# Two planes by expert for the results of an expert layer, each read back when its own tiles have landed

## What is computed

```python
x = x + tanh(g_xattn[0]) * _L0_xattn_ref(...)
x = x + tanh(g_ffn[0])   * _L0_ffn_ref(...)
x = x + tanh(g_xattn[1]) * _L1_xattn_ref(...)
x = x + tanh(g_ffn[1])   * _L1_ffn_ref(_layernorm(x), W_gate, b_gate, W_e, b_e)

def _L1_ffn_ref(x, W_gate, b_gate, W_e, b_e):
    logits = x @ W_gate + b_gate
    _, top_idx = jax.lax.top_k(logits, 2)
    y_all = jax.nn.relu(jnp.einsum('bsd,edh->bseh', x, W_e) + b_e)
    return jnp.take_along_axis(y_all, top_idx[..., None], axis=2).mean(axis=2)
```

## Time and profile before

| | us |
|---|---|
| runs shown | 986.0, 989.31, 989.25 |
| their median | 989.25 |
| the profiled execution, its own time | 989.37 |
| its span, first to last instruction | 987.3 |
| PE busy in it | 896.6 |
| DVE busy in it | 617.9 |

### The profile page before, as it was taken

How to read it: one execution, slowest core, us unless ns; L and a number is a source line. 1 busy time by engine, 2 the same in 40 slices (tenths; PEclk the granted TensorE clock), 3 DMA queues, 4 the chain that set the end, 5 groups by cost and what they waited for, 6 DMA issues and landing times.

```text
span 987.3 us, 13859 instructions
## 1 busy us (share of the span) xinstructions
PE 896.6 (91%) x4771; PEld 732.7 (74%) x4771; DVE 617.9 (63%) x1063; ACT 320.6 (32%) x572; POOL 409.3 (41%) x418
## 2 busy tenths in 40 slices
PE   4799999999999899999999999798999998668991
PEld 4677878978878877878977867575888885656770
DVE  5776575375674276575375665478888875875335
ACT  4423133223133224133223133012665664612330
POOL 4453342152442153352152333337765606546540
PEclk9899999999999999999999999799999996579995
DMA  8020120020020010020020020302344206323437
GB/s 306 12 76 11 33 86 1 11 86 2 33 86 1 13 54 32 33 86 1 11 80 6 1 76 1 108 1 58 101 131 144 67 2 220 128 75 118 139 128 287
DMA packets 42306, 70.13 MB, mean 71 GB/s; under 512 B 7098, under 2 KB 14843, under 8 KB 42115
## 3 DMA queue, kind: packets, MB, share of 16 engines
q1 hardware_dynamic: 37124, 56.97, 17.7%
q0 software_dynamic: 3680, 12.06, 3.6%
q10 hardware_dynamic: 1440, 0.24, 0.1%
HBM read 52.61 MB, written 10.22 MB: 64 GB/s over the span
## 4 chain that ended last, share of the span: by engine, by line
PE 76%; DVE 9%; issue 6%; POOL 5%; DMA 3%; ACT 1%; SPq 0%; POOLq 0%; DVEq 0%
PE ps L1345 17%; PE ps L1347 16%; PE ps L1346 16%; PE ps L1445 5%; PE ps L1437 5%; PE ps L1576 4%; PE ps L1453 3%; PE ps L1564 2%; POOL y_rows L639 2%; PE ps L1557 2%; POOL rows_in L630 1%; POOL k_blk L580 1%; DVE stats L894 1%; DMA rows_in<-h_rows,gather_i 1%; PE ps L1626 1%
## 5 line engine op out<-in xcount | busy, mean ns | idle before, releaser
L516 POOL TENSOR_TENSOR q_t<-rot_a,rot_b 128x512 f32<-128x512 f32 x64 | 82.7, 1292 | 155.2 <-DVE rot_b L944 155.2
L1345 PE MATMUL ps<-wo_hi,at_hi 128*128 128x512 f32 x256 | 107.2, 419 | 5.4 <-DVE at_lo L1013 5.4
L942 DVE TENSOR_TENSOR rot_a<-ps,cos 128x512 f32<-128x512 f32 x80 | 55.2, 690 | 89.6 <-PE ps L1347 89.4
L1345 PE MATMUL ps<-xt_hi,wq_hi 128*128 128x512 f32 x256 | 108.1, 422 | 0.2 <-issue 0.2
L1347 PE MATMUL ps<-xt_hi,wq_lo 128*128 128x512 f32 x256 | 101.5, 397 | 0.0
L1346 PE MATMUL ps<-xt_lo,wq_hi 128*128 128x512 f32 x256 | 101.4, 396 | 0.0
L1347 PE MATMUL ps<-wo_hi,at_lo 128*128 128x512 f32 x256 | 100.8, 394 | 0.0
L1346 PE MATMUL ps<-wo_lo,at_hi 128*128 128x512 f32 x256 | 100.3, 392 | 0.0
L748 ACT ACTIVATE ps<-ps 128x512 f32<-128x512 f32 x64 | 37.2, 582 | 177.7 <-PE ps L1437 177.7
L759 ACT ACTIVATE at_hi<-ps 128x512 fp32r<-128x512 f32 x64 | 38.2, 598 | 172.9 <-PE ps L1453 172.9
L1018 DVE TENSOR_TENSOR X<-ps,X 128x512 f32<-128x512 f32 x64 | 44.2, 691 | 77.8 <-PE ps L1347 77.4
(11 more groups left out here) (215 smaller groups left out, 2131.6 us busy)
## 6 DMA issues: line engine op xcount, KB each, us to landing
wq_raw<-in_wq SPq DMA_DIRECT2D x8, 1024.0 KB, 5.3
wo_raw<-in_wo SPq DMA_DIRECT2D x8, 1024.0 KB, 5.1
w_raw<-in_we SPq DMA_DIRECT2D x8, 1024.0 KB, 5.6
y_in<-y_rows SPq DMA_DIRECT2D x16, 256.0 KB, 5.6
X<-in_x SPq DMA_DIRECT2D x4, 512.0 KB, 13.1
wk_raw<-in_wk SPq DMA_DIRECT2D x8, 256.0 KB, 2.8
q_t<-in_ctx_t SPq DMA_DIRECT2D x2, 1024.0 KB, 10.5
wv_raw<-in_wv SPq DMA_DIRECT2D x4, 512.0 KB, 3.8
```

The source lines that it names most:

```text
L516: nc.gpsimd.tensor_tensor(dst, rot_a[:, r % 2, :], rot_b[:, r % 2, :], ALU.add).then_inc(rope_ok, 1)
L942: nc.vector.tensor_tensor(heads(rot_a[:, r % 2, :]), heads(bank), bcast(cos[:, :], 4), ALU.mult)
L1345: nc.tensor.matmul(dst, w_hi, x_hi, start=start and k == 0, stop=False)
```

## The change

Each row now has its two results in planes by expert: plane 0 takes that of the lower numbered of its two experts, plane 1 that of the higher. `slot2` is therefore made from the sum of a row's two slots, their maximum, and the difference of the two. Plane 0 never gets a row from expert 7.

For each of the two planes and each of the three semaphores `y_out[j]`, DVE works out how far the semaphore must have counted (`real`, `real_f`, `real_i`), behind `of_tile_i` and ahead of the remainders of the expert weights. SP loads the six numbers and waits on `y_out` itself; `landed` and `y_seq` are gone from POOL. SP reads plane 0 in 4 DMAs of 512 KB when tiles 0 to 18 have landed, and plane 1 in 8 of 256 KB when tiles 0 to 20 have. DVE adds plane 0 to all eight blocks, then plane 1 to all eight.

The core of the diff (the numbers of the waits on `slot_ok` behind it are one higher):

```diff
-            sp.wait_ge(real_ok, CREDIT + 1)
-            real = sp.value_load(last_real[0:1, 0:1], min_val=CREDIT + TOP * N // P, max_val=CREDIT + NT)
-            sp.wait_ge(y_seq, real)
+            sp.wait_ge(real_ok, CREDIT + TOP + 2)
+            lower_done, all_done = tiles_up_to(0), tiles_up_to(1)
+            for j in range(3):
+                sp.wait_ge(y_out[j], lower_done[j])
             for q in range(KT):
-                for b in range(2 * q, 2 * q + 2):
-                    for k in range(TOP):
-                        sp.dma_start(y_in[:, b, k, :], yv[:, b, k, :]).then_inc(y_ok[q], 16)
+                sp.dma_start(y_in[:, 2 * q:2 * q + 2, 0, :], yv[:, 2 * q:2 * q + 2, 0, :]).then_inc(yl_ok[q // 2], 16)
+            for j in range(3):
+                sp.wait_ge(y_out[j], all_done[j])
+            for b in range(B):
+                sp.dma_start(y_in[:, b, 1, :], yv[:, b, 1, :]).then_inc(y_ok[b // 2], 16)
...
-            def landed(i):
-                gp.wait_ge(y_out[i % 3], 16 * (i // 3) + 16)
-                gp.sem_inc(y_seq, 1)
...
-            nc.vector.tensor_tensor(of_rank[:, :, :, :], rank[:, :, :].unsqueeze(2).to_broadcast([P, B, TOP, EX]), by_rank,
-                                    ALU.is_equal).then_inc(slot_ok, 1)
...
-            nc.vector.tensor_tensor(of_rank[:, :, :, :], of_rank[:, :, :, :], slot[:, :, :].unsqueeze(2).to_broadcast([P, B, TOP, EX]),
-                                    ALU.mult).then_inc(slot_ok, 1)
-            ve.wait_ge(slot_ok, CREDIT + 8)
-            nc.vector.tensor_reduce(slot2[:, :].rearrange("p (b k) -> p b k", b=B), of_rank[:, :, :, :], AX.X, ALU.add).then_inc(slot_ok, 1)
+            nc.vector.tensor_tensor(slot[:, :, :], slot[:, :, :], sel[:, :, :].bitcast(F32), ALU.mult).then_inc(slot_ok, 1)
+            ve.wait_ge(slot_ok, CREDIT + 7)
+            by_expert = slot2[:, :].rearrange("p (b k) -> p k b", b=B)
+            nc.vector.tensor_reduce(both[:, :], slot[:, :, :], AX.X, ALU.add).then_inc(slot_ok, 1)
+            nc.vector.tensor_reduce(by_expert[:, 1, :], slot[:, :, :], AX.X, ALU.max).then_inc(slot_ok, 1)
             ve.wait_ge(slot_ok, CREDIT + 9)
+            nc.vector.tensor_tensor(by_expert[:, 0, :], both[:, :], by_expert[:, 1, :], ALU.subtract).then_inc(slot_ok, 1)
...
-            nc.vector.tensor_scalar(last_real[:, :], t_upto[:, EX - 1:EX], float(CREDIT), None, ALU.add).then_inc(real_ok, 1)
...
+            for n in range(TOP):
+                nc.vector.tensor_scalar(real[:, n, :], tile_no, t_upto[:, EX - TOP + n:EX - TOP + n + 1], 16.0, ALU.is_lt, ALU.mult).then_inc(real_ok, 1)
+            ve.wait_ge(real_ok, CREDIT + TOP)
+            nc.vector.tensor_reduce(real_f[:, :, :], real[:, :, :].rearrange("p k (n j) -> p k j n", j=3), AX.X, ALU.add).then_inc(real_ok, 1)
+            ve.wait_ge(real_ok, CREDIT + TOP + 1)
+            nc.vector.tensor_copy(real_i[:, :], real_f[:, :, :].rearrange("p k j -> p (k j)")).then_inc(real_ok, 1)
...
             for b in range(B):
-                ve.wait_ge(y_ok[b // 2], 64)
+                ve.wait_ge(yl_ok[b // 4], 32)
                 nc.vector.scalar_tensor_tensor(X[:, b, :], y_in[:, b, 0, :], tanh_g[:, 3:4], X[:, b, :], ALU.mult, ALU.add).then_inc(y0_ok, 1)
+            for b in range(B):
+                ve.wait_ge(y_ok[b // 2], 32)
                 ve.wait_ge(y0_ok, CREDIT + b + 1)
                 nc.vector.scalar_tensor_tensor(X[:, b, :], y_in[:, b, 1, :], tanh_g[:, 3:4], X[:, b, :], ALU.mult, ALU.add).then_inc(x4_ok, 1)
```

More of the change, by code:

```diff
@@ L207, in flamingo_gated_two_layers @@
         t_upto = sb("t_upto", [P, EX])
-        last_real = sb("last_real", [P, 1], I32)
+        real = sb("real", [P, TOP, NC])
+        real_f = sb("real_f", [P, TOP, 3])
+        real_i = sb("real_i", [P, TOP * 3], I32)
         slot = sb("slot", [P, B, EX])
         slot2 = sb("slot2", [P, B * TOP])
+        both = sb("both", [P, B])
         above = sb("above", [P, B * TOP])
@@ L308, in flamingo_gated_two_layers @@
                                 [sem(f"y_ok{j}") for j in range(KT)])
-        y_seq, real_ok = sem("y_seq"), sem("real_ok")
+        real_ok, yl_ok = sem("real_ok"), [sem(f"yl_ok{j}") for j in range(2)]
         tr_mm, gh_ok, glo_ok, y0_ok = sem("tr_mm"), sem("gh_ok"), sem("glo_ok"), sem("y0_ok")
@@ L455, in _, with tiles_up_to @@
             yv = y_rows[0:TOP * N].rearrange("(k b p) d -> p b k d", k=TOP, b=B)
-            sp.wait_ge(real_ok, CREDIT + 1)
-            real = sp.value_load(last_real[0:1, 0:1], min_val=CREDIT + TOP * N // P, max_val=CREDIT + NT)
-            sp.wait_ge(y_seq, real)
-            for q in range(KT):
-                for b in range(2 * q, 2 * q + 2):
-                    for k in range(TOP):
-                        sp.dma_start(y_in[:, b, k, :], yv[:, b, k, :]).then_inc(y_ok[q], 16)
+            def tiles_up_to(n):
+                few = (n + 1) * N // P
+                return [sp.value_load(real_i[0:1, 3 * n + j:3 * n + j + 1], min_val=16 * ((few - j + 2) // 3), max_val=16 * ((NT - j + 2) // 3))
+                        for j in range(3)]
+            sp.wait_ge(real_ok, CREDIT + TOP + 2)
+            lower_done, all_done = tiles_up_to(0), tiles_up_to(1)
+            for j in range(3):
+                sp.wait_ge(y_out[j], lower_done[j])
+            for q in range(KT):
+                sp.dma_start(y_in[:, 2 * q:2 * q + 2, 0, :], yv[:, 2 * q:2 * q + 2, 0, :]).then_inc(yl_ok[q // 2], 16)
[3 more added lines that the diff above has]
+                sp.dma_start(y_in[:, b, 1, :], yv[:, b, 1, :]).then_inc(y_ok[b // 2], 16)
             for b in range(B):
@@ L642, in _ @@
             gp.wait_ge(hrow_out, 16 * B)
-            gp.wait_ge(slot_ok, CREDIT + 18)
+            gp.wait_ge(slot_ok, CREDIT + 19)
             for i in range(3):
                 fetch_rows(i)
-            gp.wait_ge(slot_ok, CREDIT + 21)
+            gp.wait_ge(slot_ok, CREDIT + 22)
             for i in range(NT):
@@ L652, in _ @@
                 put_rows(i)
[L653 to L656, removed]
         @block.scalar
@@ L1249, in _ @@
                                     bounds[:, 0:EX].unsqueeze(1).to_broadcast([P, EX, EX]), ALU.is_gt).then_inc(slot_ok, 1)
+            ve.wait_ge(slot_ok, CREDIT + 2)
+            nc.vector.tensor_reduce(t_e[:, :], filled, AX.X, ALU.add).then_inc(slot_ok, 1)
             ve.wait_ge(slot_ok, CREDIT + 3)
-            nc.vector.tensor_reduce(t_e[:, :], filled, AX.X, ALU.add).then_inc(slot_ok, 1)
-            ve.wait_ge(slot_ok, CREDIT + 4)
             earlier = rank_a[:, 1, :, :]
             nc.vector.tensor_tensor(earlier, lower[:, :, :], t_e[:, :].unsqueeze(1).to_broadcast([P, EX, EX]), ALU.mult).then_inc(slot_ok, 1)
+            ve.wait_ge(slot_ok, CREDIT + 4)
+            nc.vector.tensor_reduce(t_before[:, :], earlier, AX.X, ALU.add).then_inc(slot_ok, 1)
             ve.wait_ge(slot_ok, CREDIT + 5)
-            nc.vector.tensor_reduce(t_before[:, :], earlier, AX.X, ALU.add).then_inc(slot_ok, 1)
-            ve.wait_ge(slot_ok, CREDIT + 6)
             ve.wait_ge(rank_mm, CREDIT + 2)
@@ L1269, in _ @@
                                     ALU.is_ge).then_inc(slot_ok, 1)
[L1270 removed]
+            ve.wait_ge(slot_ok, CREDIT + 11)
             nc.vector.tensor_reduce(above[:, :], reached, AX.X, ALU.add).then_inc(slot_ok, 1)
[L1272 removed]
+            ve.wait_ge(slot_ok, CREDIT + 12)
             nc.vector.scalar_tensor_tensor(slot_lo[:, :], above[:, :], -float(P), slot2[:, :], ALU.mult, ALU.add).then_inc(slot_ok, 1)
             nc.vector.tensor_tensor(reached[:, :, 0:NC], reached[:, :, 0:NC], reached[:, :, 1:NC + 1], ALU.subtract).then_inc(slot_ok, 1)
[L1275 removed]
+            ve.wait_ge(slot_ok, CREDIT + 14)
             nc.vector.tensor_tensor(tile_hot[:, :, :], reached[:, :, 0:NC], entry.unsqueeze(2).to_broadcast([P, B * TOP, NC]),
@@ L1286, in _ @@
             nc.vector.tensor_scalar(listed[:, :], ps[:, 3, 128:128 + NC], -1.0, None, ALU.add).then_inc(slot_ok, 1)
-            ve.wait_ge(slot_ok, CREDIT + 16)
+            ve.wait_ge(slot_ok, CREDIT + 17)
             nc.vector.tensor_tensor(row_of[:, :], listed[:, :], second[:, :], ALU.add).then_inc(slot_ok, 1)
-            ve.wait_ge(slot_ok, CREDIT + 17)
+            ve.wait_ge(slot_ok, CREDIT + 18)
             nc.vector.tensor_scalar(gather_i[:, :], row_of[:, :], 0.0, None, ALU.max).then_inc(slot_ok, 1)
@@ L1695, in _ @@
             turn_in(0)
-            pe.wait_ge(slot_ok, CREDIT + 24)
+            pe.wait_ge(slot_ok, CREDIT + 25)
             for i in range(NT):
```

21 lines of the change are left out of this document (9 added, 12 removed).

## The result

The changed kernel takes 982.48 us (median; 980.57 to 984.68) beside 988.26 for the kernel before; the ratio is 0.9944, its 95% interval 0.9923 to 0.9965. Measured again, beside other runs of the kernel before, it was 0.9940 (0.9919 to 0.9960). So it is faster by 0.56%, about 5.5 us.

A forecast was written before the change was run, and what follows sets the result against it. The last stretch was taken as bound by the read back, sixteen additions on DVE and the last write; 7.7 - 0.4 (writes) - 0.2 (slots) - 0.4 (fetch 22) = 6.7 us off 989.37 gave 982.6, range 979.5 to 987.2.

The forecast's parts named there:

- the sum: Whole kernel: 7.7 us saved on DVE, less writes 0.4, slots 0.2 and fetch 0.4, gives 6.7 us faster.
- the forecast case: Whole kernel: it takes 982.6 us, its own range 981.5 to 984.2; chance 0.64.
- the rival with the late plane 1: End: scatter 20 lands 2 us later amid plane 0's transfer; 0.5 to 1.5 us more, 983.1 to 984.1; chance 0.10.
- DVE's idle time and the pairs: DVE's last additions: 6.85 us of idle time and 8 x 0.12 of dependent pairs go, 7.7 us less.
- Plane 0 hidden: Plane 0's early reads: landed at 964.9, first half wanted at 966.2, so DVE doesn't wait.
- Fetch 22: Fetch of tile 22 shares the DMA engines with plane 0's reads: 0.4 us lost, bounds 0 to 4.9.
- The starved fetch: Rival: plane 0's 2.1 MB go ahead of tile 22's fetch, 4.5 us more than the sum, 987.1; chance 0.16.
- tile 22 turned later: Sign on PE: tile 22's turning at most 0.4 us later against tile 21, with a wait for `rows_in` ahead.
- Slots: DVE's slot operations: four replace two, 0.85 us instead of 0.64, so 0.2 more on the path.
- counts: DVE's counts of real tiles: 0.9 us more, taken up by its 1.32 us wait for the first tile.
- Plane 1's start: SP's second wait ends at 963.8 plus 0.1, data from 964.9, last of it by 973.3 at 311 GB/s.
- The writes: Last writes at the end, 0.67 us apart, may queue: 0.4 us for the last, bounds 0 to 1.5.

The follow-up runs named there:

- the paced run: Changed kernel with plane 1 read in 4 DMAs of 512 KB and at most two of plane 0's 512 KB reads in flight; ratio 0.9948 to the kernel before.

## Why the prediction was right, and where its terms were off

The time was forecast at 982.6, 6.7 us faster; it is 982.48, and by the ratio 5.5 faster. That the two times agree within 0.1 us is luck: the saving came out 1.2 us smaller than forecast, and the kernel before, with a median of 988.26 over five runs, 1 us faster than the median of three that the sum stood on. Two steps of the forecast case were off, and what came is nearer to the rival with the late plane 1, which was priced at a saving 0.5 to 1.5 us smaller than the sum. (A slip besides: 989.37 less 6.7 is 982.7, not 982.6. And "no other engine works in that stretch" isn't quite what the rows show, for the relu and scatter 22 run there; they are not on the path.)

- **DVE's idle time and the pairs** (7.7 us): right. From the end of the bias of tile 22 to the last addition 11.1 us, forecast 10.8; the difference is the wait in plane 1. With plane 1 left out it is 10.6. How much of this reaches the end is another matter: the paired order costs 3.3 us by the timed runs and 1.4 to 1.8 by the profiles.
- **Plane 0 hidden**: right. Issued at 952.95, 4.9 us ahead of scatter 20, and DVE never waits for it.
- **Fetch 22** (0.4): 0.54 in this profile, shown by the run that reads plane 0 behind it, and 0.2 to 1.0 in the others with the same early reads. The starved fetch didn't come; in the paced run, where reads were in flight for longer, it cost 1.4. The sign that I had named, tile 22 turned later, is not how it showed. The fetch, issued at 951.37, landed after 4.5 us, and only the load of its rows into PE waited, by 0.32. The turning itself starts 0.27 ahead of the bias of tile 20, as it did before (0.31), but the product behind it comes 0.85 behind its start instead of 0.36. Changed kernel first, then the kernel before:

```profile
955.95 0.42 PEld L1680 LDWEIGHTS ps<-ident,rows_in 128*128 128x128 f32 x4 [0.32 <-DMA rows_in<-h_rows,gather_i]
956.80 0.50 PE L1353 MATMUL ps<-w_hi,gx_hi 128*128 x1 [0.20 <-issue]
...
959.57 0.48 PE L1345 MATMUL ps<-w_hi,gx_hi 128*128 x1
```

- **Slots** (0.2) and **counts** (hidden): right. The slots take 0.84 us, from the product to the comparison, forecast 0.85. The counts take 0.64 more, forecast 0.9, and DVE's wait for tile 0 shrinks from 1.32 to 0.83, so they are hidden:

```profile
858.43 0.22 DVE L1260 TENSOR_TENSOR slot<-slot,sel 128x64 f32<-128x64 f32 x1
...
859.27 0.58 DVE L1269 TENSOR_TENSOR r_d<-slot,route 128x400 f32<-128x400 f32 x1
...
868.63 3.75 DVE L1206 TENSOR_TENSOR w_lo<-w_raw,w_hi 128x512 fp32r<-128x512 f32 x6
873.21 0.69 DVE L1314 TENSOR_TENSOR gx_lo<-ps,gx_hi 128x512 fp32r<-128x512 f32 x1 [0.83 <-ACT gx_hi L872]
```

- **Plane 1's start**: wrong. The step was "SP's wait ends at 963.8 plus 0.1", 2.8 us behind the issue of scatter 20. It was 5.2 to 5.4. I took the 2.66 us of a scatter with nothing beside it for one beside 2.1 MB of reads. The rival with the late plane 1 named this, and priced it at 0.5 to 1.5 us.
- **The writes** (0.4): mis-sized. They cost 1.7: 4.20 behind the last addition against 2.49. The term counted the writes' own queue (0.25, with plane 1 left out), and took plane 1 as landed by 973.3 at 311 GB/s. It started 2.6 later and went at 217 GB/s for its first 5 us; then it and the writes went at 404 to the end.

So in the changed kernel's profile the end behind the bias of tile 22 is 5.7 us shorter (21.7 to 16.0); less 0.54 and 0.2 that is 5.0, where the sum had 6.7. The 1.7 are 1.3 of writes and 0.4 of the wait in plane 1 (0.1 and 0.2 less when run again).

What the three parts of the change are worth one by one is shown only roughly. The span behind the issue of scatter 20 goes from 26.2 us to 24.4 with the direct wait, to 22.3 with the early plane 0 and paired additions, and to 21.0 and 20.5 with all of it: 1.8, 2.1, and 1.4 to 1.8. The ratios of the timed runs give 0.8, 1.4 and 3.3, each uncertain by some 2 us.

What bounds the new end is settled in part. It is not the issuing queue. The DMA engines move 404 GB/s without a gap until 976.5, so the bytes behind the landing of the last real tile set the last stretch; but without any of plane 1's bytes the end would still come 14.0 us behind the start of the bias of tile 22 (the run without plane 1), for the additions and one write, where it comes 16.0 and 15.7 behind it. So plane 1's bytes cost 1.6 to 2.0 us there, and DVE's additions remain the larger part. Every edit that let plane 1 start earlier left more to move behind it, and those edits are all at 0.9948 to 0.9951. What stays open is why reads of `y_rows` start slowly. In the first 5 us behind SP's first read for which it waited for all tiles, all queues together moved 242 GB/s in the kernel before, 217 and 257 in two profiles of the changed kernel and 194 to 277 in the others with plane 1, with the scatters of padding and without, with 256 KB and with 512 KB, from one queue and from two; only the paced kernel, with part of plane 0 still moving, had 318. No run here was faster than the changed kernel beyond its interval.

## What to carry to other kernels

When results are read back behind a last transfer, ask what else is in flight when that transfer is issued: an early read that is free for the engine that consumes it can hold up the write that everything waits for. Ordering the work so that the consumer always has something to do (eight additions while the second plane arrives) was worth 1.4 to 3.3 us here. A direct wait that started the transfer 3 us sooner brought 0.8 (timed) to 1.8 (profile) by itself, and starting the second plane sooner still brought nothing. Price a tail by the bytes that have to drain behind the last dependence, at the rate that the trace shows for that mix, and not by one engine's queue alone.

## What the runs showed of the hardware

A scatter from POOL's queue is held up by reads that SP issued ahead of it. Issued beside four reads of 512 KB it landed in 5.3 us instead of 2.7, and where it was issued 0.5 us behind the last of them it moved 0.02 MB in 4.8 us, while SP's queue moved 1.55. It isn't starved for as long as SP's queue has work, though. In the changed kernel scatter 19 was issued at 953.30, just behind the first read, and landed 6.9 us later. Traffic from 956 to 958 and from 958 to 960:

```profile
q1 hardware_dynamic: 348, 0.68, 96.7%
...
q1 hardware_dynamic: 291, 0.56, 72.4%
q0 software_dynamic: 80, 0.26, 32.2%
```

First it moves nothing, then all of its 0.26 MB, while half of plane 0 is still moving. It began when about 0.9 MB of the reads had moved, and scatter 20, issued behind all four reads, when about 1.9 MB had, here and in the kernel that reads plane 0 behind the fetch. That would fit a service in the order of issue; no run here tests it.

The Trainium skill (DMA: Bandwidth & Descriptors, Queues, rings and completion order) has each DMA engine take turns, packet by packet, between the queues that it has work for. By that rule a scatter should have had a good share from its first packet on; the trace agrees for 958 to 960 and doesn't for the wait ahead of it, so for this kernel the measurement decides.

The stretches of 392 to 404 GB/s on one core, reads and writes mixed, lie above the 358 that the same page gives per core (Specifications). Its section on bandwidth has up to 425 GB/s for one core whose neighbour is idle, and the trace lies between the two.
